# A two-layer graph network: the second layer's chain and table in two parts, its midpoint and output in three, x loaded whole

## The reference, cut to what matters

```python
h = jnp.maximum(_layernorm(x), 0.0)
x = x + _L0_gnn_ref(h, adj, weight, bias, node_w, edge_w)   # attention over the neighbours
h = jnp.maximum(_layernorm(x), 0.0)
x = x + _L1_gnn_ref(h, adj, W)                              # the layer that the change touches
```

```python
mx = h @ W
res = tanh(|mx| / |h| * artanh(|h|)) * (mx / |mx|)           # 0 where |mx| is tiny
gamma = max(2 / (1 - |res|^2), 1e-15)
denom, nom = clamp_abs(adj @ (gamma - 1)), adj @ (gamma * res)
two_mean = nom / denom
a_mean = two_mean / (1 + sqrt(max(1 - |two_mean|^2, 1e-10)))
AXW = tanh(sum(adj, row) * artanh(|a_mean|)) * a_mean / |a_mean|
out = x + expmap0(relu(logmap0(AXW)))
```

## Time and profile before

| | us |
|---|---|
| median of 3 runs (lowest, highest) | 778.36 (775.69, 782.87) |
| the profiled execution, device time | 774.91 |
| its span | 773.3 |
| busy: PE, DVE, ACT, POOL | 500.3, 445.9, 340.0, 389.8 |
| POOL, the 160 gathers of the second layer, busy | 156.6 |
| second layer's products (L1438), busy | 115.7 |

### The profile page before, as it was taken

The page is one execution under the profiler, slowest core; times in us unless marked ns, Lnnn a source line. Parts: engine busy times, 40 slices in busy tenths (PEclk is TensorE's granted clock), DMA queues, the critical chain, the costliest instruction groups (busy, mean ns, idle before and its releaser), DMA issues.

```text
span 773.3 us, 12413 instructions
## 1 busy us (share of the span) xinstructions
PE 500.3 (65%) x3644; PEld 415.9 (54%) x3644; DVE 445.9 (58%) x1790; ACT 340.0 (44%) x706; POOL 389.8 (50%) x447
## 2 busy tenths in 40 slices
PE   4767463758797777879688778920676667555520
...
GB/s 320 269 252 158 186 263 361 303 289 273 295 259 305 127 343 210 262 295 208 79 76 99 47 1 1 2 85 182 106 102 103 106 103 104 103 103 103 103 23 218
...
## 3 DMA queue, kind: packets, MB, share of 16 engines
...
...
## 4 chain that ended last, share of the span: by engine, by line
PE 25%; DVE 18%; issue 14%; DMA 13%; ACT 11%; POOL 11%; DVEq 4%; ACTq 2%; POOLq 1%; SPq 1%
POOL work L1387 10%; PE bank L821 7%; DMA work<-in_adj 7%; PE bank L1438 7%; ACT work L617 4%; DMA front<-in_x 4%; PE bank L760 3%; PE bank L1565 2%; PE bank L792 2%; DVE gx L1614 2%; DVEq L1210 2%; ACT work L1451 1%; DVE work L1097 1%; DVE fs L1053 1%; DVE front L1021 1%
## 5 line engine op out<-in xcount | busy, mean ns | idle before, releaser
L715 POOL DMA_INDIRECT work<-table_h,work x160 | 166.1, 1038 | 102.7 <-issue 72.9
L1387 POOL DMA_INDIRECT work<-table_y,idx x160 | 156.6, 979 | 100.5 <-DMA table_y<-work 52.1
L1438 PE MATMUL bank<-work 128*128 128x257 f32 x320 | 115.7, 531 | 91.7 <-issue 48.1
L617 ACT ACTIVATE work<-work 128x2048 bf16<-128x2048 f32 x64 | 121.8, 1903 | 57.2 <-PE bank L760 27.6
L1438 PEld LDWEIGHTS bank<-work 128*128 128x128 f32 x320 | 82.9, 269 | 114.1 <-issue 50.2
L821 PE MATMUL bank<-work 128*128 128x128 f32 x640 | 96.4, 313 | 14.9 <-DVEq L1099 14.9
L821 PEld LDWEIGHTS bank<-work 128*128 128x128 f32 x640 | 90.3, 225 | 17.0 <-DVEq L1099 14.5
L1455 ACT ACTIVATE work<-bank 128x257 f32 x32 | 12.4, 386 | 176.3 <-PE bank L1438 176.3
L1401 DVE TENSOR_SCALAR work<-work 128x640 bf16<-128x640 f16 x32 | 13.0, 405 | 131.5 <-PE bank L1432 131.2
L760 PE MATMUL bank<-work 128*128 128x256 bf16 x512 | 73.8, 297 | 21.9 <-ACT work L617 21.9
L760 PEld LDWEIGHTS bank<-work 128*128 128x128 bf16 x512 | 52.2, 106 | 39.2 <-ACT work L617 28.3
...
## 6 DMA issues: line engine op xcount, KB each, us to landing
...
work<-table_h,work POOLq DMA_INDIRECT x160, 4.5
work<-table_y,idx POOLq DMA_INDIRECT x160, 2.8
```

What stands on the lines that cost most here:

```text
L617: a.activation(abf[:, h, :], adu[:, b % 2, h, :], ACT.Copy, accum_out=cnt[:, k, b, h:h + 1]).then_inc(L["conv"], 1)
L715: p.indirect_dma_start(gat[:, k, n, :], None, table_h, bass.IndirectOffsetOnAxis(ix[:, k, n:n + 1], 0)) \
L1387: p.indirect_dma_start(gt2[:, k, n % GT, :], None, table_y, bass.IndirectOffsetOnAxis(idx[:, n:n + 1], 0)) \
L1438: last = t.matmul(bank[4 + b % 2][:, 0:DY], otf[:, b % 2, q, :], gt2[:, k, b * TILES + q, 0:DY], start=(q == 0), stop=(q == TILES - 1))
```

## The change

There are three parts. Line numbers of the changed file differ from those of the profile; where rows of its order stand below, the sentence ahead says which lines they are.

**x loaded whole.** The buffer `xs` and its semaphore `x_used` are gone. All eight groups of x are loaded into their places in `gx` (as `x1`), which the products overwrite only after the group was normed, and all are issued ahead of the front loop: three before the first load of adj, two behind it, three behind the weights and before the second load of adj.

**Moebius chain and table in two parts.** The chain is run for blocks 0 to 19 (EARLY_M) when group 4 has been squared: its first answer stands between the second and the third block of group 5 on ACT, its second behind group 5. The chain for blocks 20 to 31 (LATE_M) follows the last group. Of the groups, DVE scales 0, 2, 4, then 5 and 7, POOL 1 and 3, ACT 6. The lengths' answers move one group ahead on ACT.

**Midpoint and output in three parts.** `midpoint_dve` and `midpoint_act` take a slice of columns and a phase. Blocks 0 to 19 (FIRST) go through it at blocks 21 to 24 of the gather loop and are scaled, added and stored at blocks 25 to 29; blocks 20 to 27 (THEN) at blocks 29 to 31, added by POOL behind its gathers; blocks 28 to 31 (LAST) behind the loop. The loops over blocks on DVE and ACT are written out. PE's loop and the gathers are not changed.

```diff
+            def load(g):
+                e.dma_start(x1[:, grp(g), :], x_r[:, grp(g), :]).then_inc(f0.x_in[g], 16)
+            load(0)
             e.dma_start(ew, edge_w.rearrange("(c p) d -> p c d", p=P)).then_inc(s_w, 16)
             e.dma_start(nw, node_w.rearrange("(c p) d -> p (c d)", p=P), allow_slow_non_contiguous=True).then_inc(s_w, 16)
-            load(1, 1)
+            load(1)
+            load(2)
             load_block(e, 0, 0)
+            load(3)
+            load(4)
...
+            for g in range(5, NG):
+                load(g)
...
-                    load(g + 2, g % 2)
...
-                    front_norm(a, f0, xs[:, k, :, :], g, k)
-                    a.drain().then_inc(f0.x_used, 1)
+                    front_norm(a, f0, x1[:, grp(g), :], g, k)
...
+        EARLY_M, LATE_M = slice(0, 20), slice(20, NB)
+        def mobius_dve(d, c, phase):
+            if phase == 0:
...
+                pose(d)
+            if phase == 1:
+                hear(d)
...
+                pose(d)
...
+            if phase == 2:
+                hear(d)
...
+        def mobius_act(a, c, phase):
+            if phase == 0:
+                answer(a, MN[:, c], S2[:, c], ACT.Sqrt, ACT.Tanh)
+            if phase == 1:
+                answer(a, TH[:, c], Z[:, c], ACT.Tanh, ACT.Sqrt)
...
+        FIRST, THEN, LAST = slice(0, 20), slice(20, 28), slice(28, NB)
+        AT_FIRST, AT_THEN, AT_OUT = 21, 29, 25
         def fm_dve(d):
             d.sem_inc(F["m"], 2)
             d.wait_ge(F["const"], 1)
 
...
+            def mask(n):
+                d.wait_ge(F["t"], n + 1)
+                then(d, d.tensor_scalar(mm1, iow2, last_e[:, n:n + 1], None, ALU.is_lt))
+                d.scalar_tensor_tensor(mm2[:, n % 2, :], iow2, first_e[:, n:n + 1], mm1, ALU.is_ge, ALU.mult)
+                d.drain().then_inc(F["m"], 1)
+            def measured(n):
                 d.wait_ge(F["nomc"], n + 3)
                 squares(d, n)
+            for n in range(NB):
+                mask(n)
+                if n >= 2:
+                    measured(n - 2)
+                if 0 <= n - AT_FIRST < 4:
+                    midpoint_dve(d, FIRST, n - AT_FIRST)
+                if n - AT_FIRST == 3:
+                    d.drain().then_inc(F["u"], 1)
+                if 0 <= n - AT_OUT < 5:
+                    for b in range(GB):
+                        add_x(d, GB * (n - AT_OUT) + b, F["us"], F["o"])
+                if 0 <= n - AT_THEN < 3:
+                    midpoint_dve(d, THEN, n - AT_THEN)
+            measured(NB - 2)
+            midpoint_dve(d, THEN, 3)
+            d.drain().then_inc(F["u"], 1)
+            measured(NB - 1)
+            for phase in range(4):
+                midpoint_dve(d, LAST, phase)
+            d.drain().then_inc(F["u"], 1)
+            for n in range(LAST.start, NB):
+                add_x(d, n, F["us"], F["o"])
+        def add_x(d, n, ready, done):
+            d.wait_ge(ready, n + 1)
+            d.tensor_tensor(x1[:, n, :], nom[:, n, 0:D], x1[:, n, :], ALU.add).then_inc(done, 1)
+        def scaled_relu(a, n, done):
+            a.activation(nom[:, n, 0:D], nom[:, n, 0:D], ACT.Relu, scale=F3[:, n:n + 1]).then_inc(done, 1)
+        def fm_out_pool(p):
+            for n in range(THEN.start, THEN.stop):
+                add_x(p, n, F["us"], F["o_pool"])
+        def fm_out_sp(e):
+            for g in range(NG):
+                if GB * g < FIRST.stop:
+                    e.wait_ge(F["o"], GB * (g + 1))
+                elif GB * g < THEN.stop:
+                    e.wait_ge(F["o_pool"], GB * (g + 1) - THEN.start)
+                else:
+                    e.wait_ge(F["o"], GB * (g + 1) - (THEN.stop - THEN.start))
+                e.dma_start(out_r[:, grp(g), :], x1[:, grp(g), :]).then_inc(F["out"], 16)
...
+            a.activation(tab[:, :], eps_t[:, :], ACT.Sqrt)
+            for n in range(NB):
+                a.wait_ge(F["t"], n + 3)
+                a.wait_ge(F["nom"], n + 2 * GB - 1)
+                a.activation(otf[:, n % 2, :, :],
+                             bank[6 + n % 2][:, :].bitcast(BF16)[:, 0:EW].rearrange("p (q n) -> p q n", q=TILES),
+                             ACT.Copy).then_inc(F["tc"], 1)
+                if 0 <= n + 1 - AT_FIRST < 3:
+                    midpoint_act(a, FIRST, n + 1 - AT_FIRST)
+                if 0 <= n + 1 - AT_OUT < 5:
+                    a.wait_ge(F["u"], 1)
                     for b in range(GB):
...
+                        scaled_relu(a, GB * (n + 1 - AT_OUT) + b, F["us"])
+                if 0 <= n + 1 - AT_THEN < 3:
+                    midpoint_act(a, THEN, n + 1 - AT_THEN)
+                if n == NB - 1:
+                    a.wait_ge(F["u"], 2)
+                    for b in range(GB):
+                        scaled_relu(a, THEN.start + b, F["us"])
+                a.wait_ge(F["nom"], n + 2 * GB + 1)
+                a.activation(nom[:, n, :], bank[4 + n % 2][:, 0:DY], ACT.Copy)
+                a.drain().then_inc(F["nomc"], 1)
+            for b in range(GB):
+                scaled_relu(a, THEN.start + GB + b, F["us"])
+            for phase in range(3):
+                midpoint_act(a, LAST, phase)
+            a.wait_ge(F["u"], 3)
+            for n in range(LAST.start, NB):
+                scaled_relu(a, n, F["us"])
...
+        def midpoint_dve(d, c, phase):
+            if phase == 0:
+                d.drain()
...
+                pose(d)
+            if phase == 1:
+                hear(d)
...
+                pose(d)
+            if phase == 2:
+                hear(d)
...
+                pose(d)
...
+            if phase == 3:
+                hear(d)
...
+        def midpoint_act(a, c, phase):
+            if phase == 0:
+                answer(a, col[:, R14, c], col[:, S14, c], ACT.Sqrt, ACT.Ln)
+            if phase == 1:
+                answer(a, col[:, TA, c], col[:, U2, c], ACT.Ln, ACT.Tanh)
+            if phase == 2:
+                answer(a, col[:, TA, c], col[:, NN, c], ACT.Tanh, ACT.Sqrt)
...
+        SCALED_BY = {"dve": (0, 2, 4, 5, 7), "pool": (1, 3), "act": (6,)}
 
         def table_sp(e, B):
             for g in range(NG):
+                by = [name for name in SCALED_BY if g in SCALED_BY[name]][0]
+                e.wait_ge(B.ys[by], SCALED_BY[by].index(g) + 1)
                 e.dma_start(ty_r[:, grp(g), :], ys[:, g, :, :]).then_inc(B.tyo, 16)
+        def scale_rows(v, B, by, g):
+            for b in range(GB):
+                n = g * GB + b
+                v.tensor_scalar(ys[:, g, b, 0:D], mx[:, n, :], GR[:, n:n + 1], None, ALU.mult)
+            v.tensor_copy(ys[:, g, :, D], GM1[:, g * GB:g * GB + GB])
+            v.drain().then_inc(B.ys[by], 1)
...
+            p.wait_ge(B.gm, 1)
+            for g in SCALED_BY["pool"]:
+                scale_rows(p, B, "pool", g)
...
+                    if g == 5 and b == 1:
+                        mobius_act(a, EARLY_M, 0)
...
+                if g in (2, 3):
+                    lengths_act(a, g - 2)
+                if g == 5:
+                    mobius_act(a, EARLY_M, 1)
             a.drain().then_inc(B.sq, 1)
+            for phase in range(2):
+                mobius_act(a, LATE_M, phase)
+            a.wait_ge(B.gm, 2)
             a.wait_ge(B.ysz, 1)
+            for g in SCALED_BY["act"]:
...
+            lengths_dve(d, 0)
+            norm_columns(d, f, 4)
+            lengths_dve(d, 1)
+            norm_columns(d, f, 5)
+            lengths_dve(d, 2)
+            norm_columns(d, f, 6)
+            d.wait_ge(f.prod_used, 5)
+            mobius_dve(d, EARLY_M, 0)
+            mobius_dve(d, EARLY_M, 1)
+            norm_columns(d, f, 7)
+            mobius_dve(d, EARLY_M, 2)
             d.drain().then_inc(B.gm, 1)
             d.wait_ge(B.ysz, 1)
...
+            for g in (0, 2, 4):
+                scale_rows(d, B, "dve", g)
+            d.wait_ge(B.sq, 1)
+            for phase in range(3):
+                mobius_dve(d, LATE_M, phase)
+            d.drain().then_inc(B.gm, 1)
+            for g in (5, 7):
+                scale_rows(d, B, "dve", g)
```

225 lines of the change are left out of this document (76 added, 149 removed).

## The result

The changed kernel takes 754.94 us (median of 4 runs, 754.43 to 757.89), the kernel before 779.08 us (775.69 to 782.87) beside it: a ratio of 0.970, 95% interval 0.9645 to 0.975. The forecast was 757 us in a range of 747 to 767. The profiled execution took 754.43 us, its span is 752.8 us at a mean granted clock of 0.82.

What follows compares the result with a forecast made beforehand. Bounds: waits for x behind SP's queue, chain and stores before the gathers, POOL's gathers, an end without overlap. 5.0 + 6.6 - 2.2 + 9.7 = 19.1 us off 774.9 gives 755.8, median put at 757; range 747 to 767.

Steps and rivals of the forecast that it cites:

- Front, 5.0 us: Loading x whole: DVE's later waits for x go, a late first store delays ACT's group 2; 5.0 us gained.
- The rival in which the front gains all: Front: queue not served in order, store lands in time, 12.5 us gained, 749.5 us in all; chance 0.10.
- Table, 6.6 us: Chain and table in parts: early stores are away before the late chain ends, first gather starts 6.6 us earlier.
- The bound for twice the price, 3.4 us: Table: if POOL's scaling costs twice its add, group 3 is ready at 517.3 and the gain is 3.4 us.
- Gathers, 2.2 us lost: Gather loop: 26 us more DVE work beside POOL's gathers costs them 8.5% of it, 2.2 us.
- End, 9.7 us: Behind the gathers: only four blocks' chain and relus remain, so the end comes at 763.6 instead of 773.3.
- The delay ahead of it: Tail: ACT's second-part answer and table load make its copy, and so the last chain, 1.8 us later.
- Two of the signs: Signs of being right: first gather 11 to 12 us earlier in the span; 160 gathers near 0.99 us.
- The rival with POOL shut out (784 us): Gather loop: DVE's chains and adds hold POOL for their whole length, 29 us instead of 2.2; chance 0.03.

Runs made afterwards that it cites:

- e5: Changed kernel with the first table_h store issued before the second adj load and x of groups 4 to 7, weights behind the fourth store: 749.88 us, 0.967 of before.
- e2: Changed kernel with one Moebius chain over all 32 blocks and the scaling on DVE and ACT only: 763.87 us, 0.986 of before.
- e3: Changed kernel with midpoint and output in one part on all 32 blocks behind the loop: 766.35 us, 0.988 of before.
- e8: Changed kernel with 108 more fp32 copies on DVE, six for each of blocks 2 to 19, beside POOL's gathers: 755.87 us, 0.971 of before.
- e7: Changed kernel without POOL's eight additions of x for blocks 20 to 27, whose output lacks it: 759.10 us, 0.974 of before.
- e1: Changed kernel with x loaded on demand again, group g+2 behind the table_h store of group g: 764.68 us, 0.985 of before.
- e12: Changed kernel with ACT's last steps reordered, no late table loads, additions on DVE instead of POOL: 754.02 us, 0.966 of before.

## Why the prediction was right

The forecast of 757 us holds: 754.94 and 756.75 in two comparisons. By its steps:

- **Front, 5.0 us.** 5.9 measured. The first store landed at 31.3, as worked out (31.4), and held the norm of group 2; that its landing waits behind the bytes issued before it is what e5 shows, by taking them away: 12.1 us from issue to landing become 6.9, and the front gains 6.7 more. Not foreseen was that the store would also be issued 8.6 us late (19.21 against 10.57); the landing did not suffer, since the bytes ahead of it set it. The rival in which the front gains all had the size that e5 reached by another order (85.2 against 97.7, 12.5 us) and the wrong condition.
- **Table, 6.6 us.** 6.6 measured, and 7.1 lost when undone (e2). One input was off: POOL scales a row in about 1.0 us, not 0.735. Group 3 was ready near 511 all the same, because POOL began at 502.58 where 504.7 was worked out. The two errors cancelled, which was luck. (The bound for twice the price, 3.4 us, comes out at 3.7 by the terms given: 517.3, five stores of 1.6 and 2.6 make 527.9. The forecast does not use it.)
- **Gathers, 2.2 us lost.** Wrong in the term, small in the sum: the stretch was 203.0 and 202.4 us against 204.1, with 17.5 us more DVE work in it. I had read all the excess of the mean gather over 0.945 us as DVE's doing, and e3 and e8, with 58.0 and 104.9 us of DVE work there, both took 205.8 us: no slope stands out of a scatter of 4.5 us.
- **End, 9.7 us.** 11.3 and 9.1 in the two profiles, 9.6 by e3. The last part ran 3.66 + 6.38 = 10.0 us to its last answer (9.8 predicted), 1.7 to the relus (1.8) and 7.0 to the end (7.1). The delay ahead of it was put at 1.8 us; it was 0.2 in one profile and 2.5 in the other (last gather to first operation 7.59 and 9.87, before 7.41). ACT's late copies cost nothing in the first, since PE's last products had to wait for the last gather's landing anyhow (3.55 us behind it, before 3.58); in the second they cost 0.3 us, and the halved clock of these products 2.2. The term lies between the two and was met by neither. Missed was that POOL's additions, which I had costed at nothing since they are done in time, slow DVE's first operations: 1.1 us (e7).
- **First layer.** No term, rightly: of its 4.4 us more in the first profile, 3.6 came also with x as before (e1, 375.5), and nearly all went with x whole (e5, e12: 372.2 and 373.3).

Two of the signs did not come as written: the first gather stood 8.1 us earlier in the span and not 11 to 12, the first layer's 4.4 us being in between, and the mean gather was 972 ns and not near 990. The rival with POOL shut out (784 us) is excluded by the run, and by e8 that all of DVE's work is added to the gathers. The prediction also read the Trainium skill's page SBUF — State Buffer, section "SBUF: two separate sides", too widely: beside a GpSimd DMA that section names operations on two ports, and it lists operations with two inputs, such as the 20 additions, as locking only against a GpSimd operation that reads SBUF. The sum of the measured stretches, 20.5 us, is near the 19.1 of the forecast in part by luck, because the gathers' error of 3.3 us and the first layer's 4.4 us stand against each other.
